# Loading and splitting the picked heads' weights in the second attention's last period, and their first products in front of its last projection back

## The reference, cut to what matters

```python
x = x + _L1_attn_ref(_L1_cond_ref(x, ...), g_norm, W_qkv, W_out, pm)     # third: the second attention
x = x + _L1_ffn_ref(_L1_cond2_ref(x, itok_B_0_15, fc1_w, fc1_b, fc2_w, fc2_b, experts_w, experts_b), ...)

def _L1_cond2_ref(x, indices, fc1_w, fc1_b, fc2_w, fc2_b, experts_w, experts_b):
    h = gelu(einsum('bnd,hd->bnh', x, fc1_w) + fc1_b, approximate=False)      # 256 -> 1024
    shared = einsum('bnh,sh->bns', h, fc2_w) + fc2_b                          # 192 columns
    expert_x = einsum('bnh,bph->bnp', h, experts_w[indices]) + experts_b[indices][:, None, :]   # 64 picked
    return concatenate([shared, expert_x], axis=-1)
```

## Time and profile before

| | us |
|---|---|
| median of 3 runs (2564.64 to 2568.38) | 2566.94 |
| the profiled execution's own time | 2556.43 |
| its span | 2554.6 |
| TensorE busy in the span | 2376.6 (93%) |
| VectorE, ScalarE, GpSimd busy | 1845.0, 1258.8, 1016.4 |
| mean granted clock of TensorE | 0.969 of full speed |

### The profile page before, as it was taken

One profiled execution on the slowest core, in us unless ns is written; L12 is line 12 of the kernel. 1 busy time (PEld: TensorE's weight loads), 2 busy tenths in 40 slices (PEclk: granted clock), 3 DMA queues, 4 the chain that ended last, 5 costly groups with the idle time before them and its releaser, 6 DMA issues.

```text
span 2554.6 us, 54443 instructions
## 1 busy us (share of the span) xinstructions
PE 2376.6 (93%) x18880; PEld 2106.9 (82%) x18880; DVE 1845.0 (72%) x5107; ACT 1258.8 (49%) x3774; POOL 1016.4 (40%) x1074
## 2 busy tenths in 40 slices
PE   4799999999995799999999999799999999999898
PEld 3577878878774688888888887799999999999898
DVE  5777777777768566666667665478778888888566
ACT  2566565666652355555555555333325555555322
POOL 4545445454533444454454444023222222221243
PEclk7899999999987899999999999899999999999999
DMA  4321212112120222112211221312135777777323
GB/s 118 100 47 46 55 45 57 45 41 51 34 90 2 65 50 54 48 44 53 54 45 45 54 52 38 95 35 42 35 109 202 234 227 235 236 225 230 106 75 116
DMA packets 153078, 225.70 MB, mean 88 GB/s; under 512 B 54294, under 2 KB 123174, under 8 KB 142054
## 3 DMA queue, kind: packets, MB, share of 16 engines
q1 hardware_dynamic: 143942, 203.56, 27.4%
q0 software_dynamic: 8864, 18.66, 2.8%
HBM read 159.32 MB, written 27.16 MB: 73 GB/s over the span
## 4 chain that ended last, share of the span: by engine, by line
PE 69%; DVE 10%; issue 8%; ACT 7%; POOL 3%; DMA 1%; SPq 1%; POOLq 0%; ACTq 0%; DVEq 0%
PE bank L55 53%; PE bank L136 7%; PE bank L321 2%; PE bank L1203 2%; ACT P L1385 2%; PE bank L348 1%; PE bank L1244 1%; ACT Ph L597 1%; DVE xe L860 1%; ACT PTh L609 1%; ACT L1433 1%; POOL P L1644 1%; PE bank L431 1%; DVE xe L863 1%; DVE Ph L746 1%
## 5 line engine op out<-in xcount | busy, mean ns | idle before, releaser
L1385 ACT ACTIVATE P<-P,mx 128x144 f32<-128x144 f32 x512 | 206.3, 404 | 345.0 <-DVE mx L1489 345.0
L55 PE MATMUL bank<-xD_hi,w1e_lo 128*128 128x256 f32 x880 | 254.6, 289 | 1.9 <-issue 1.9
L55 PE MATMUL bank<-w2e_hi,hrD_lo 128*128 128x256 f32 x880 | 250.9, 285 | 5.4 <-issue 5.4
L55 PE MATMUL bank<-w2e_hi,hrD_hi 128*128 128x256 f32 x880 | 251.1, 285 | 4.7 <-issue 4.5
L55 PE MATMUL bank<-xD_hi,w1e_hi 128*128 128x256 f32 x880 | 249.9, 284 | 2.8 <-issue 2.8
L55 PE MATMUL bank<-xD_lo,w1e_hi 128*128 128x256 f32 x880 | 250.0, 284 | 2.4 <-issue 2.4
L55 PE MATMUL bank<-w2e_lo,hrD_hi 128*128 128x256 f32 x880 | 250.6, 285 | 1.3 <-issue 1.3
L2418 POOL DMA_INDIRECT xE<-d_y,ixs x78 | 110.5, 1416 | 343.8 <-PE bank L136 316.9
L1049 POOL TENSOR_TENSOR xe<-xe 128x704 f32<-128x704 f32 (+3 forms) x64 | 87.3, 1363 | 400.0 <-DVE xe L865 399.7
L2051 ACT ACTIVATE hD<-bank,b1E 128x256 f32<-128x256 f32 x312 | 128.6, 472 | 199.3 <-PE bank L55 190.5
L2122 DVE CAST hrD_hi<-hD 128x512 fp32r<-128x512 f32 x284 | 121.4, 427 | 138.9 <-ACT hD L2051 114.9
(11 more groups left out here) (316 smaller groups left out, 7818.5 us busy)
## 6 DMA issues: line engine op xcount, KB each, us to landing
w1raw<-in_ew SPq DMA_DIRECT2D x39, 1024.0 KB, 5.9
w2raw<-in_ew SPq DMA_DIRECT2D x39, 1024.0 KB
K<-Kn SPq DMA_DIRECT2D x256, 72.0 KB, 2.1
Q<-Qn SPq DMA_DIRECT2D x256, 64.0 KB, 2.0
d_ys<-oE SPq DMA_DIRECT2D x39, 256.0 KB
d_rot<-QK SPq DMA_DIRECT2D x16, 512.0 KB, 2.9
Rs<-d_rot SPq DMA_DIRECT2D x64, 128.0 KB, 4.2
b2E<-in_eb SPq DMA_DIRECT2D x39, 128.0 KB, 3.6
```

What stands on the lines that cost most here:

```text
L55: inst = e.matmul(out, l, r, start=k == 0, stop=k == len(pairs) - 1)
L1385: inst = e.activation(P1[t % 2][:, n, :], P1[t % 2][:, n, :], ACT.Exp, bias=mx1[t % 2][:, 2 * g + sg:2 * g + sg + 1], scale=-1.0, accum_ou ...
```

## The change

It has five parts.

1. Tiles are laid out anew. w1 goes to the end of the second attention's stage, the tiles of the first stages are reordered so that those in w1's new place are the ones whose readers it already waits for, and the tiles of stage d that are loaded early (f1, f2a, their raw tiles, f20, f2raw0) come to lie on w1. f1b, f2b, wr, sb2, eb, xD and hD move to room that is kept. No instruction or wait of the earlier stages changes with it.
2. `sync_d` starts f1raw (twice), f2araw and f2raw0's shared columns as soon as p_V1 = 64 (the last product that reads w1 is done) and SP has started the last stacking of Q and K; then, once those have landed, the small tables and `load_picked(0)`. f2raw1's shared columns and `load_picked(1)` come after v_back = 16, as before.
3. The three pieces are no longer rounded by ACT. VectorE makes both parts of each (`picked_weights`), in steps 3, 4 and 5 of period 15, and the two parts of X of batch 0 (`picked_x(0)`) in step 6, each time behind `copy_turned` of that step.
4. TensorE does `picked_up(0, 0)` and `picked_up(0, 1)`, 24 products, in step 1 of period 16, in front of `back(15, 0)`; the rest of batch 0's first layer comes after `back(15, 1)`.
5. The last projection back writes bank 6 in place of bank 1, and waits for the last maxima, which read that bank.

```diff
         def sync_d(e):
-            e.wait_ge(v_back, B)
-            for dst, src in ((f1b, "f1b"), (f2b, "f2b"), (wr, "wr")):
-                e.dma_start(dst, a[src]).then_inc(l_d, 16)
-            e.dma_start(sb2, a["sb2"].broadcast_to((128, 256))).then_inc(l_d, 16)
+            e.wait_ge(p_V1, 4 * B)
             for i in range(2):
                 e.dma_start(f1raw[i], a["f1"][:, :, 512 * i:512 * i + 512]).then_inc(l_dw[i], 16)
             e.dma_start(f2araw, a["f2a"]).then_inc(l_dw[2], 16)
-            for i in range(2):
-                e.dma_start(f2raw[i][:, :, 0:64], a["f2c"]).then_inc(l_f2c, 16)
+            e.dma_start(f2raw[0][:, :, 0:64], a["f2c"]).then_inc(l_f2c, 16)
+            for half in range(2):
+                e.wait_ge(l_st[half][(B - 1) % 2], stacked(B - 1, half))
+            for dst, src in ((f1b, "f1b"), (f2b, "f2b"), (wr, "wr")):
+                e.dma_start(dst, a[src]).then_inc(l_d, 16)
+            e.dma_start(sb2, a["sb2"].broadcast_to((128, 256))).then_inc(l_d, 16)
...
             load_picked(0)
+            e.wait_ge(v_back, B)
+            e.dma_start(f2raw[1][:, :, 0:64], a["f2c"]).then_inc(l_f2c, 16)
             load_picked(1)
...
+        def picked_weights(e, i):                    # VectorE
+            dst, src, c = fixed_d[i]
+            cols = slice(c, c + src.shape[2])
+            e.wait_ge(l_dw[i], LW + 16)
+            e.tensor_copy(dst[0][:, :, cols], src).then_inc(*vs.up())
+            e.wait_ge(s_v, vs.n)
+            e.tensor_tensor(dst[1][:, :, cols], src, dst[0][:, :, cols].bitcast(F32), ALU.subtract).then_inc(v_w1, 1)
...
                     if b == -2 and s < 6:
                         split_weights(s)
+                    if b == B - 1 and 3 <= s < 6:
+                        picked_weights(e, s - 3)
+                    if b == B - 1 and s == 6:
+                        picked_x(e, 0)
...
                     if s == 1:
                         project(b + 1, 2)
+                    if b == B and s == 1:
+                        picked_up(e, 0, 0)
+                        picked_up(e, 0, 1)
                     if s == 2:
                         back(b - 1, 0)
...
             for i in range(STEPS + 1):
-                up(i, 0)
-                up(i, 1)
+                if i:
+                    picked_up(e, i, 0)
+                    picked_up(e, i, 1)
                 turn_y(i - 2)
                 turn_rows(i + 1 - B)
-                up(i, 2)
-                up(i, 3)
+                picked_up(e, i, 2)
+                picked_up(e, i, 3)
...
-            for i, (dst, src, c) in enumerate(fixed_d):          # ScalarE
-                e.wait_ge(l_dw[i], LW + 16)
-                e.activation(dst[0][:, :, c:c + src.shape[2]], src, ACT.Copy).then_inc(c_w1, 1)
             e.wait_ge(l_d, LD + 64)
-            e.wait_ge(l_f2c, 32)
...
-            split_x(0)                                           # VectorE
-            for i, (dst, src, c) in enumerate(fixed_d):
-                cols = slice(c, c + src.shape[2])
-                e.wait_ge(c_w1, WD + i + 1)
-                e.tensor_tensor(dst[1][:, :, cols], src, dst[0][:, :, cols].bitcast(F32), ALU.subtract).then_inc(v_w1, 1)
```

More of the change, by code:

```diff
@@ L1145, in program, with back_bank @@
         proj_bank = (0, 1, 1, 0, 0, 1, 0, 1)
+        def back_bank(b):
+            return halves(6 if b == B - 1 else 1)
         def sync_c(e):
@@ L1588, in add_back @@
                 e.wait_ge(p_back, 2 * b + 2)
-                e.tensor_tensor(X[:, b], halves(1), X[:, b], ALU.add).then_inc(v_back, 1)
+                e.tensor_tensor(X[:, b], back_bank(b), X[:, b], ALU.add).then_inc(v_back, 1)
             def split_weights(c):
@@ L1704, in program @@
         TILES = B + NT
+        f1b, f2b, wr, sb2 = kept("f1b", 8), kept("f2b", 2), kept("wr", 2, 8), kept("sb2", 256)
+        eb = [kept(f"eb{i}", 2) for i in range(2)]
+        xD = [[kept(f"xD{i}_{x}", 2, 256, dt=F32R) for x in ("hi", "lo")] for i in range(2)]
+        hD = kept("hD", 4, 256)
         LG, upper, iota8 = kept("LG", 32, 8), kept("upper", 128), kept("iota8", 8)
@@ L1723, in program @@
         stage.append(ctx.enter_context(ExitStack()))
+        zi = tile("zi", 256, dt=I32)
+        yD, yrD = [tile(f"yD{i}", 2, 256) for i in range(2)], [tile(f"yrD{i}", 2, 256) for i in range(2)]
+        f2, f2raw = [None, pair("f21", 8, 128)], [None, tile("f2raw1", 8, 128)]
+        tile("space2", 32)
         f1, f2a = pair("f1", 2, 1024), pair("f2a", 8, 128)
-        f1b, f2b, sb2, wr = tile("f1b", 8), tile("f2b", 2), tile("sb2", 256), tile("wr", 2, 8)
         f1raw, f2araw = [tile(f"f1raw{i}", 2, 512) for i in range(2)], tile("f2araw", 8, 128)
-        f2, f2raw = [pair(f"f2{i}", 8, 128) for i in range(2)], [tile(f"f2raw{i}", 8, 128) for i in range(2)]
-        eb, zi = [tile(f"eb{i}", 2) for i in range(2)], tile("zi", 256, dt=I32)
-        yD, yrD = [tile(f"yD{i}", 2, 256) for i in range(2)], [tile(f"yrD{i}", 2, 256) for i in range(2)]
+        f2[0], f2raw[0] = pair("f20", 8, 128), tile("f2raw0", 8, 128)
         next_stage()
@@ L1784, in sync_d @@
         def sync_d(e):
-            e.wait_ge(v_back, B)
+            e.wait_ge(p_V1, 4 * B)
+            for i in range(2):
+                e.dma_start(f1raw[i], a["f1"][:, :, 512 * i:512 * i + 512]).then_inc(l_dw[i], 16)
+            e.dma_start(f2araw, a["f2a"]).then_inc(l_dw[2], 16)
+            e.dma_start(f2raw[0][:, :, 0:64], a["f2c"]).then_inc(l_f2c, 16)
+            for half in range(2):
+                e.wait_ge(l_st[half][(B - 1) % 2], stacked(B - 1, half))
             for dst, src in ((f1b, "f1b"), (f2b, "f2b"), (wr, "wr")):
@@ L1924, in sync_e, with picked_up @@
             e.wait_ge(l_out, 16 * 32)
-        def pe_d(e):
[L1928 to L1945, removed]
+        def picked_up(e, i, n):
+            if i >= STEPS:
+                return
+            k, q = 4 * i + n, i - B
+            w = f1 if q < 0 else w1e[weights_of(q) % 2]
+            e.wait_ge(v_x, i + 1)
+            if i == 0:
+                e.wait_ge(v_w1, WD + n // 2 + 1)
+                e.wait_ge(c_V1, 4 * B)
+                if n == 1:
+                    e.wait_ge(v_back, B - 1)
+            elif q >= 0:
+                e.wait_ge(v_w1, WE + weights_of(q) + 1)
+            if k >= 4:
+                e.wait_ge(c_g, k - 3)
+            for m in range(2):
+                f = 2 * n + m
+                inst = matmuls3(e, halves(n)[:, m, :], [
+                    (cut(w, lambda x: x[:, k_, f * 128:f * 128 + 128]), cut(xD[i % 2], lambda x: x[:, k_, :]))
+                    for k_ in range(2)])
+            inst.then_inc(p_up, 1)
+        def pe_d(e):
             def turn_x(b):
@@ L1951, in turn_x @@
                     e.wait_ge(v_R, b)
+                else:
+                    e.wait_ge(v_back, B)
                 if b >= B - 2:
@@ L2058, in picked_high @@
                 e.wait_ge(l_e[b % 2], 32 * (b // 2 + 1))
-                if b >= 2:
+                if b < 2:
+                    e.wait_ge(l_f2c, 16 * b + 16)
+                else:
                     e.wait_ge(p_down, b - 1)
@@ L2110, in act_d, with picked_x @@
                     gates()
+        def picked_x(e, b):
+            if b >= B:
+                return
+            if b >= 2:
+                e.wait_ge(p_up, 4 * (b - 1))
+            elif b == 0:
+                for half in range(2):
+                    e.wait_ge(l_st[half][(B - 1) % 2], stacked(B - 1, half))
+            e.tensor_copy(xD[b % 2][0], X[:, b]).then_inc(*vs.up())
+            e.wait_ge(s_v, vs.n)
+            e.tensor_tensor(xD[b % 2][1], X[:, b], xD[b % 2][0].bitcast(F32), ALU.subtract).then_inc(v_x, 1)
+        def picked_weights(e, i):
[3 more added lines that the diff above has]
+            e.tensor_copy(dst[0][:, :, cols], src).then_inc(*vs.up())
+            e.wait_ge(s_v, vs.n)
+            e.tensor_tensor(dst[1][:, :, cols], src, dst[0][:, :, cols].bitcast(F32), ALU.subtract).then_inc(v_w1, 1)
         def dve_d(e):
@@ L2356, in dve_d @@
                 logits(i - 2)
[L2357 removed]
+                picked_x(e, i + 1)
                 rows(q + 1)
```

38 lines of the change are left out of this document (14 added, 24 removed).

## The result

The changed kernel took 2549.98 us in the median of four runs (2547.7 to 2558.45), the kernel before 2565.79 beside it; the ratio is 0.9944 [0.9923, 0.9965], which is -14.4 us [-19.8, -9.0]. The forecast was -8.0.

A forecast was written before the change was run, and what follows sets the result against it. TensorE, busy in 93% of the span, was taken as the bound, with time to win only where it idles or runs at low clock; 5.4 - 20.7 + 4.25 + 2.0 + 1.0 = -8.0 us from 2566.9 gave 2559.0, range 2554 to 2565.

The forecast's parts named there:

- Loads: Early start of f1 and f2a loads: 5.88 us of load and 1.9 us of SP issues leave the chain, waits cost nothing.
- Splits on DVE: Steps 3 to 6 of period 15: step 3 costs 0, then +1.33, +1.86 and +1.06; sum +4.25 us.
- From the projection to up(1, 0): Seam after the last projection back: DVE is the chain, 5.4 us in place of 20.7.
- First products: 24 products ahead of the last projection back: 2.86 us less 0.84 idle, so the projection starts +2.0 us later.
- Clock: Tail of the loop of heads: one fall of TensorE's clock, +1.0 us taken, bounds 0 and 1.7.
- the rival with the slower tail: Clock low from steps 5 and 6 through half the projection: about +4 us more, result -4.0, 2563.0; chance 0.20.

The follow-up runs named there:

- before_gap64: The kernel before with one gap of 64 bytes ahead of w1raw0 and nothing of the change: -21.8 us against the kernel before.
- again: The changed kernel run once more with no edit, for a second profile: 2555.56 us, -12.1 us against the kernel before.
- late_pieces: Changed kernel with first piece and X split in step 3 of period 15, second and third piece in step 1 of period 16: -19.8 us against the kernel before.
- best: Changed kernel with later second and third piece, first piece and X in step 3, plus 64-byte shifts of w2e against hrD: 2526.55 us, -38.5 against the kernel before.
- layout_only: The kernel before with the new tile places only; loads, splits, order of products and bank as before: -5.1 us against the kernel before.
- order_only: Changed kernel with small gaps that bring back the old distances of xD to w1e and f1 and of xr to w1: +1.5 us against the kernel before.
- dist_back: Changed kernel with a 64-byte gap behind hD, putting xD and w1e a multiple of 256 bytes apart again: -2.3 us against the kernel before.
- w2e_64: Changed kernel with w2e moved by 64 bytes against hrD, gaps elsewhere meant to keep the other distances: -28.8 us against the kernel before.
- w2e_128: Changed kernel with w2e at 128 bytes from hrD, by gaps of 32, 32 and 32: -11.6 us against the kernel before.

## Why the prediction was wrong

**Loads: right.** f1raw was started at 1574.65 and nothing waited for it. **Splits on DVE: right.** The copy took 0.68 (0.68 taken). Step 3 cost nothing. Turnings came at 1595.81, 1600.82 and 1604.87. From step 4's to step 5's it was 1.31 us longer than before (1.33 forecast), then steps of 5.01 and 4.05, 4.85 and 4.05 forecast.

**From the projection to up(1, 0): right.** 1620.7 to 1626.21 is 5.5 us (5.4). **First products: right in kind.** Behind or in front was worth +1.1 forecast, +1.1 and +1.9 measured, neither clear of the noise. (24 products at the spacing of the earlier trace rows are 2.82 us and not 2.86, which changes nothing.)

**Clock: the mis-sized term.** I took 1.0; in the changed kernel's profile it came to an estimated 4.3 to 4.5. Of that, 0.7 lies in step 1 (a fall that before_gap64, with the old order, has as well, and again has not), 0.15 in step 5, 0.6 ahead of the last values, 0.8 in them, and 2.2 in the 24 products, which took 5.05 in place of 2.86 us. The seam alone says the same: -9.0 without the clock was forecast, -4.7 came out. This is the rival with the slower tail, nearly to the number (-4.0 with its 5 us of clock). In all seven profiles with the splits in steps 4 to 6 the clock was at 1.2 GHz for 13 us or more between step 4 and the end of the last projection; in late_pieces and best it was not there at all between 1580 and 1619. Over all profiles the seam is 74.9 us in the mean of the four kernels with the old order (72.9 to 76.5) and 69.3 in the mean of the six with the changed one (68.9 to 69.7): -5.5. Two of those four with the old order, layout_only and before_gap64, had a fall of 3 to 7 us at the projection as well, so the old order does not keep the clock up either. By itself this term would have made the change smaller than forecast, so it is not why the time fell below the range.

**The layout: the step that failed.** My working began at the loads. The first of the five parts of the change, the new places of the tiles, got no price at all. The premise behind that was "time can only be won where TensorE stands still, or where it runs at its lower clock", and "what is won ahead of that stretch shifts all that follows" took the time inside the stretch as fixed. Both failed: TensorE won time where it never stood still and ran at full clock. The routed stretch got 0.84% shorter, an estimated 5.3 us over the stage's 5280 products, and the picked heads 0.6 us in each of two filled stretches of 400 products (47.2 to 46.6). layout_only shows such a gain by itself (-5.1), and order_only and dist_back take most or all of it away.

Together with -5.5 at the seam that is about -12, and -12.1 and -14.4 were measured; but this agreement is in part luck. The sum counts only what got shorter. The 400 products around the stall near 1684 took 2.6 us more in the two profiles of the changed kernel than in the two of the kernel before, products 13200 to 13600 took 2.4 more, those behind the routed stretch 3.0. As wholes, the two profiled executions of the changed kernel are only 1.1 us shorter (2557.8 and 2558.9 in the mean).

The Trainium skill (TensorE: Matmul & The Clock Gate, Back-to-back issue gap) says that the spacing of products in a stream is set by the weight load and the product together; the runs fit that, in that the place of the one's tile relative to the other's moved the spacing, from 120 to 114 ns. By the formula that the Trainium skill gives there for the isolated gap at full clock, 256 columns would take an estimated 109 ns; the best measured here is 113.3, the mean in the routed stretch of w2e_64.

**What stays open.** The parts do not add up in the timed runs. The distance alone is worth 5.1 in the old order (layout_only) and 9.8 (dist_back) or 13.6 (order_only) in the new one, and the seam's -5.5 is not seen where the distance is 0. Kernels with both layers at distance 0 ran 5 to 10 us slower in timed runs than when profiled (order_only 2570.3 and 2564.8, dist_back 2565.3 and 2554.9); before_gap64 ran 7 faster (2545.6 and 2552.8). It may be that a distance of 0 costs more without the profiler, but this is not shown: each kernel has one profiled execution or two, and dist_back's timed runs spread from 2555.9 to 2572.5. The stall near 1684, 8 to 11 us for ten products in most kernels and 6 to 7 before, was not tested by itself either.

## What to carry to other kernels

A change that moves tiles has a price even if not one instruction changes: work out the distance, modulo 256 bytes, of each streamed tile to the tile that TensorE loads as weights for it, before and after, and compare starts of products in a stretch that TensorE fills. Work put into an idle engine is free only outside the loop that the idle time belongs to: DVE looked half idle in steps 5 and 6, but everything put there was paid in full (steps of 5.01 and 4.05 us in place of 2.99), and with TensorE's longer waits its clock fell as well. Where two places are open, the one under a long run of another engine (here the 7 us of the projection) is the one to take.

## What the runs showed of the hardware that was not expected

The time in ns from one float32r product of 128 x 128 by 256 to the next at full clock, by the distance of the two tiles in bytes (streamed less loaded, modulo 256, worked out from the layouts). The distances stand in the order of the two columns. The figures are means over the routed stage of all starts less than 125 ns apart, which leaves out waits, the lower clock and the first product behind another kind:

| distance | xD with w1e | w2e with hrD | kernel |
|---|---|---|---|
| 0 and 0 | 119.9 | 120.0 | before |
| 64 and 0 | 117.8 | 119.8 | changed |
| 64 and 128 | 117.7 | 118.7 | w2e_128 |
| 192 and 64 | 115.9 | 113.7 | before_gap64 |
| 64 and 64 | 114.2 | 114.0 | w2e_64 |

In these five layouts a multiple of 256 is the slowest, 128 little better, and 64 and 192 the fastest. It is the distance and not the place of one tile: in the changed kernel w2e and hrD both lie 192 bytes beyond a multiple of 256, and their products stand at 119.8. It is also not the larger multiples that count: in order_only and dist_back xD and w1e are a multiple of 256 but not of 512 apart, and the stretch takes the same 430.32 us as in the kernel before.

The distance of the pair does not set the spacing alone. In w2e_64 the products of xD with w1e fell when only the distance of w2e changed. And the 115.9 of before_gap64 is the mean of two levels: in each batch the 24 products of xD with w1e that follow those of w2e stand at 117.9, and the 24 behind the transposes, with the same tiles, at 114 to 115. They differ in the columns of w1e, in the banks they write and in what ran just before them; no run here tells these apart.

All this is seen where TensorE has no pause; in the second attention shifts of 1 to 2 ns in the spacing changed the time of 4800 products by at most 0.4 us.
